# Softmax row sums taken from a 65th weight column of the value matmuls instead of from ScalarE's accumulator

## The reference, cut to what matters

```python
qkv = x @ W_qkv.T + b_qkv                       # 16 heads of 32
scores = einsum('bqhe,bkhe->bhqk', q, k) * scale
scores = where(causal, scores, -inf)
attn = softmax(scores, axis=-1)
out = einsum('bhqk,bkhe->bqhe', attn, v)
x = x + (out.reshape(b, l, d) @ W_out.T + b_out) + ffn(xn)
```

## Time and profile before

| | |
|---|---|
| median of 3 runs | 1747.48 us (1744.93 to 1747.74) |
| the profiled execution, its own time | 1748.79 us |
| its span, first to last instruction | 1747.0 us |
| busy over the span | PE 97%, weight load 78%, DVE 60%, ACT 42%, POOL 16% |
| first layer and start of the projection | 0 to about 641 us |
| projection | about 642 to 772 us |
| attention | about 772 to 1170 us |
| feed-forward net and output projection | about 1171 to 1747 us |

### The profile page before, as it was taken

How to read it: one execution, slowest core, us unless ns; L and a number is a source line. 1 busy time by engine, 2 the same in 40 slices (tenths; PEclk the granted TensorE clock), 3 DMA queues, 4 the chain that set the end, 5 groups by cost and what they waited for, 6 DMA issues and landing times. The chain is left out here.

```text
span 1747.0 us, 22877 instructions
## 1 busy us (share of the span) xinstructions
PE 1690.6 (97%) x8318; PEld 1365.9 (78%) x8318; DVE 1044.7 (60%) x1795; ACT 733.9 (42%) x1528; POOL 286.8 (16%) x280
## 2 busy tenths in 40 slices
PE   5999999999999989989999999989999999999998
PEld 3677888788788878867777777768888888888887
DVE  4321365564623454459999999964655654655776
ACT  4521322232213332249999999972222222222221
POOL 3201210310310112100000000013154031033220
PEclk9899999999999999989999999999999999999999
DMA  7200110110101038833445445514010010012243
GB/s 280 102 17 1 61 49 19 55 31 25 55 7 37 30 113 269 298 147 95 122 136 139 127 123 142 139 48 151 1 48 25 1 48 25 0 49 65 81 133 132
DMA packets 75663, 149.59 MB, mean 86 GB/s; under 512 B 9497, under 2 KB 26521, under 8 KB 74018
## 3 DMA queue, kind: packets, MB, share of 16 engines
q1 hardware_dynamic: 75554, 148.17, 27.0%
HBM read 101.87 MB, written 46.27 MB: 85 GB/s over the span
## 5 line engine op out<-in xcount | busy, mean ns | idle before, releaser
L1560 DVE TENSOR_TENSOR pt_lo<-p_turn,pt_hi 128x512 fp32r<-128x512 f32 (+3 forms) x384 | 200.8, 550 | 18.4 <-ACT pt_hi L1533 14.3
L1553 DVE TENSOR_REDUCE row_top<-p_score 128x1 f32<-128x128 f32 (+7 forms) x256 | 189.5, 750 | 15.5 <-PE p_score L1485 15.3
L1525 ACT ACTIVATE prob<-p_score,row_top 128x128 f32<-128x128 f32 (+7 forms) x256 | 190.0, 745 | 6.3 <-DVE row_top L1553 5.5
L1533 ACT ACTIVATE pt_hi<-p_turn 128x512 fp32r<-128x512 f32 (+3 forms) x384 | 182.5, 494 | 5.5 <-PE p_turn L1496 1.6
L1496 PE MATMUL p_turn<-ident,prob 128*128 128x128 f32 x1152 | 181.5, 276 | 1.3 <-DVE pt_lo L1560 1.0
L1019 DVE TENSOR_TENSOR hid<-hid,p_up 128x512 f32<-128x512 f32 x64 | 44.0, 688 | 218.7 <-PE p_up L484 203.0
L1896 DVE TENSOR_TENSOR e_hid<-e_hid,e_p_up 128x512 f32<-128x512 f32 x64 | 44.0, 687 | 196.2 <-PE e_p_up L1782 196.2
L1511 PE MATMUL p_o<-pt_hi,v 128*128 128x512 f32 (+3 forms) x384 | 148.6, 395 | 4.0 <-ACT o_both L1543 3.2
L1496 PEld LDWEIGHTS p_turn<-ident,prob 128*128 128x128 f32 x1152 | 131.8, 141 | 14.9 <-DVE pt_lo L1560 1.7
L1483 PE MATMUL p_score<-stack 128*128 128x512 f32 (+3 forms) x384 | 128.3, 389 | 7.1 <-PEq L54 3.5
L766 ACT ACTIVATE hid<-p_gate 128x512 f32<-128x512 f32 x64 | 38.3, 599 | 217.3 <-PE p_gate L484 217.2
(11 more groups left out here) (272 smaller groups left out, 4027.1 us busy)
## 6 DMA issues: line engine op xcount, KB each, us to landing
stack<-qk_parked SPq DMA_DIRECT2D x256, 128.0 KB, 3.9
raw<-in_wgu SPq DMA_DIRECT2D x64, 256.0 KB, 2.6
qk_parked<-qk SPq DMA_DIRECT2D x16, 1024.0 KB, 4.0
v_parked<-v_out SPq DMA_DIRECT2D x16, 512.0 KB, 5.6
v<-v_parked SPq DMA_DIRECT2D x8, 1024.0 KB, 9.4
o_parked<-o_both SPq DMA_DIRECT2D x64, 128.0 KB
res<-in_x SPq DMA_DIRECT2D x8, 512.0 KB
rot<-in_w2t SPq DMA_DIRECT2D x4, 1024.0 KB, 8.0
```

What stands on the lines that cost most here:

```text
L1525: act.activation(row_at(h, r, 0, width_of(r)), p_score[:, r % 2, 0:width_of(r)], ACT.Exp, bias=top[:, r:r + 1], accum_out=sums).then_inc(e ...
L1533: act.activation(pt_hi[:, (BL * h + j) % PT, c0:W], p_turn[:, (BL * h + j) % TB, c0:W], ACT.Copy).then_inc(rounded, 1)
L1553: dve.tensor_reduce(top[:, r:r + 1], p_score[:, r % 2, 0:width_of(r)], AX_X, ALU.max, negate=True).then_inc(topped, 1)
L1560: dve.tensor_tensor(pt_lo[:, slot, c0:W], p_turn[:, (BL * h + j) % TB, c0:W], pt_hi[:, slot, c0:W].bitcast(F32), ALU.subtract).then_inc(sp ...
```

## The change

The value tensors `v_out`, `v_parked` and `v` get 65 columns a head (`VC`): 32 high, 32 low, and one column of ones, which GpSimd writes once into `v_out`. `weigh` uses the 65 columns of the one head as weights, so row 64 of `p_o` holds the row sums of that head. `exp` accumulates nothing, `total` is gone, `read_o` copies 65 rows instead of 64, and SyncE stores the 65th by itself as `sum_parked`. In `layer_end` SyncE loads all sums in one load of 128 x 256 elements, VectorE inverts them after the third unit of the feed-forward net, and SyncE stores them; the transposes and the copy are gone. The pieces of a value store are 1040 bytes instead of 1024, those of a value load 8320 instead of 8192, and the spread loads of the last stage read 2048 bytes at a stretch instead of 512. Bias and scale of the projection are loaded at the end of `layer_zero` instead of at the start of the projection. `ORDER` stays as it is.

```diff
@@ -27,6 +27,7 @@
 HEADS, E = 16, 32
+VC = 2 * E + 1
@@ -306,6 +310,8 @@
                 sp.dma_start(ahead.raw[:, i], t["wqk"][0, i]).then_inc(ahead.loaded[i], 16)
+            sp.dma_start(ahead.bias[:], t["qk_bias"]).then_inc(ahead.consts, 16)
+            sp.dma_start(ahead.scale[:, 0:1], t["qk_scale"]).then_inc(ahead.consts, 16)
@@ -1205,16 +1210,16 @@
-            sp.dma_start(bias[:], qk_bias).then_inc(consts, 16)
-            sp.dma_start(scale[:], qk_scale).then_inc(consts, 16)
...
             for m in range(NT):
+                if m == 0:
+                    sp.wait_ge(one_set, 2)
...
                 b, tb = divmod(m, S // P)
-                to = v_dram.rearrange("(q b) p n -> b p q n", b=B)[b, :, :, tb * 8 * E:(tb + 1) * 8 * E]
-                sp.dma_start(to, v[:, m % BANKS].rearrange("p q h a e -> p q (h a e)").bitcast(F32))\
+                to = v_dram.rearrange("(q b) p n -> b p q n", b=B)[b, :, :, tb * 4 * VC:(tb + 1) * 4 * VC]
+                sp.dma_start(to, v[:, m % BANKS].rearrange("p q h c -> p q (h c)").bitcast(F32))\
@@ -1245,7 +1250,8 @@
             pool.memset(one[:], 1.0).then_inc(one_set, 1)
-            pool.wait_ge(one_set, 1)
+            pool.memset(v[:, :, :, :, 2 * E:].bitcast(F32), 1.0).then_inc(one_set, 1)
+            pool.wait_ge(one_set, 2)
@@ -1301,7 +1307,7 @@
                     act.wait_ge(v_stored[m % BANKS], 16 * (m // BANKS))
-                act.activation(v[:, m % BANKS, :, :, 0, :], p_v[:, m % BANKS].rearrange("p (q h e) -> p q h e", q=QUADS, h=4),
+                act.activation(v[:, m % BANKS, :, :, 0:E], p_v[:, m % BANKS].rearrange("p (q h e) -> p q h e", q=QUADS, h=4),
@@ -1332,15 +1338,15 @@
                 dve.wait_ge(v_rounded, m + 1)
-                dve.tensor_tensor(v[:, m % BANKS, :, :, 1, :], p_v[:, m % BANKS].rearrange("p (q h e) -> p q h e", q=QUADS, h=4),
-                                  v[:, m % BANKS, :, :, 0, :].bitcast(F32), ALU.subtract).then_inc(v_split, 1)
+                dve.tensor_tensor(v[:, m % BANKS, :, :, E:2 * E], p_v[:, m % BANKS].rearrange("p (q h e) -> p q h e", q=QUADS, h=4),
+                                  v[:, m % BANKS, :, :, 0:E].bitcast(F32), ALU.subtract).then_inc(v_split, 1)
...
-def attention(nc, mask, stack, v, ident, qk_dram, v_dram, o_dram, total, o_both, o_stored, qk_last, load_next):
+def attention(nc, mask, stack, v, ident, qk_dram, v_dram, o_dram, sum_dram, o_both, o_stored, qk_last, load_next):
@@ -1447,8 +1453,10 @@
                 row, t0 = E * (2 * pr + a), b * S + g * W
-                sp.dma_start(o_dram[it, :, row:row + E, t0:t0 + W], o_both[:, (G * h + g) % OS])\
-                    .then_inc(o_stored[(G * h + g) % OS], 16)
+                stored = o_stored[(G * h + g) % OS]
+                sp.dma_start(o_dram[it, :, row:row + E, t0:t0 + W], o_both[0:2 * E, (G * h + g) % OS]).then_inc(stored, 16)
+                sp.dma_start(sum_dram[TT * it + G * b + g, row // E:row // E + 1], o_both[2 * E:VC, (G * h + g) % OS])\
+                    .then_inc(stored, 16)
@@ -1506,10 +1514,10 @@
                 pe.wait_ge(split, BL * (HB * it + h) + j + 1)
-                lhs = v[:, b, kb, 2 * pr:2 * pr + 2].rearrange("p a h e -> p (a h e)")
+                lhs = v[:, b, kb, 2 * pr + a]
                 slot = (BL * h + j) % PT
-                pe.matmul(p_o[:, c0:W], lhs, pt_hi[:, slot, c0:W], start=(kb == 0), stop=False)
-                pe.matmul(p_o[:, c0:W], lhs, pt_lo[:, slot, c0:W], start=False,
+                pe.matmul(p_o[0:VC, c0:W], lhs, pt_hi[:, slot, c0:W], start=(kb == 0), stop=False)
+                pe.matmul(p_o[0:VC, c0:W], lhs, pt_lo[:, slot, c0:W], start=False,
@@ -1521,9 +1529,8 @@
                 wait(act, turned, BL * (HB * it + h - 2) + (r + 1 if r < QB else QB + r + 1))
-                sums = total[:, bass.ds(QB * G * 4 * (B * it + b) + 4 * r + 2 * pr + a, 1)]
                 act.activation(row_at(h, r, 0, width_of(r)), p_score[:, r % 2, 0:width_of(r)], ACT.Exp,
-                               bias=top[:, r:r + 1], accum_out=sums).then_inc(exped, 1)
+                               bias=top[:, r:r + 1]).then_inc(exped, 1)
@@ -1534,13 +1541,12 @@
             def read_o(it, h, g):
-                a = h % 2
...
                     act.wait_ge(*qk_last)
-                wait(act, o_stored[(G * h + g) % OS], 16 * (G * HB // OS * it + (G * h + g) // OS))
-                act.activation(o_both[:, (G * h + g) % OS], p_o[64 * a:64 * a + 64, :], ACT.Copy).then_inc(o_read, 1)
+                wait(act, o_stored[(G * h + g) % OS], 32 * (G * HB // OS * it + (G * h + g) // OS))
+                act.activation(o_both[:, (G * h + g) % OS], p_o[0:VC, :], ACT.Copy).then_inc(o_read, 1)
@@ -1680,8 +1685,8 @@
                 for h in range(4):
-                    to = raw[E * h:E * h + E, n % RING].rearrange("p (i n) -> p i n", i=J)
-                    sp.dma_start(to, spread[TT * quad + q, h:h + 1].to_broadcast([E, J, P])).then_inc(inv_in[n % RING], 16)
+                    sp.dma_start(raw[E * h:E * h + E, n % RING], inv_dram[TT * quad + q, h:h + 1].to_broadcast([E, W]))\
+                        .then_inc(inv_in[n % RING], 16)
@@ -1700,12 +1705,15 @@
                     load_res(k // 2 - 2)
-            sp.wait_ge(inv_copied, 1)
-            sp.dma_start(inv_dram.rearrange("(k p) n -> p k n", p=P), inv_t[:]).then_inc(inv_out, 16)
             for semaphore in o_stored:
-                sp.wait_ge(semaphore, 16 * (2 * HEADS * B // len(o_stored)))
+                sp.wait_ge(semaphore, 32 * (2 * HEADS * B // len(o_stored)))
+            sp.dma_start(inv_t[:], sum_dram.rearrange(flat, k=2)).then_inc(sums_in, 16)
             load_res(0)
-            for k in range(12, 12 * NG + QUADS):
+            for k in range(12, 24):
+                load_raw(k)
+            sp.wait_ge(inverted, 1)
+            sp.dma_start(inv_dram.rearrange(flat, k=2), inv_t[:]).then_inc(inv_out, 16)
+            for k in range(24, 12 * NG + QUADS):
@@ -1809,13 +1817,6 @@
                     hidden(u, c)
-                if u == 0:
-                    pe.wait_ge(inverted, 1)
-                    for i in range(2):
-                        mm = pe.transpose(p_out[:, 0, i * P:(i + 1) * P], total[:, i * P:(i + 1) * P], ident[:, :])
-                    mm.then_inc(inv_turned, 1)
-                if u == 1:
-                    pe.wait_ge(inv_copied, 1)
@@ -1850,8 +1851,6 @@
                     silu(1, 0)
-                    act.wait_ge(inv_turned, 1)
-                    act.activation(inv_t[:].rearrange("p k n -> p (k n)"), p_out[:, 0, 0:2 * P], ACT.Copy).then_inc(inv_copied, 1)
@@ -1931,7 +1930,6 @@
-            dve.reciprocal(total[:, :], total[:, :]).then_inc(inverted, 1)
@@ -1950,6 +1948,9 @@
                     add(u - 1)
+                if u == 2:
+                    dve.wait_ge(sums_in, 16)
+                    dve.reciprocal(inv_t[:], inv_t[:]).then_inc(inverted, 1)
@@ -1964,9 +1965,10 @@
     qk_dram = nc.dram_tensor("qk_parked", [HEADS // 2 * B, 2, P, S], F32, kind="Internal").ap()
-    v_dram = nc.dram_tensor("v_parked", [HEADS // 4 * B, P, 8 * S // P * E], F32, kind="Internal").ap()
+    v_dram = nc.dram_tensor("v_parked", [HEADS // 4 * B, P, 4 * S // P * VC], F32, kind="Internal").ap()
     o_dram = nc.dram_tensor("o_parked", [HEADS // 4, 2, P, T], F32, kind="Internal").ap()
-    inv_dram = nc.dram_tensor("inv_parked", [HEADS * NT, P], F32, kind="Internal").ap()
+    sum_dram = nc.dram_tensor("sum_parked", [HEADS, 4, W], F32, kind="Internal").ap()
+    inv_dram = nc.dram_tensor("inv_parked", [HEADS, 4, W], F32, kind="Internal").ap()
```

More of the change, by code:

```diff
@@ L79 @@
     done: object
+    bias: object
+    scale: object
+    consts: object
 def layer_zero(nc, t, ident, x_hi, x_lo, spare, half_turned, parked, raw_at, ahead):
@@ L1149, in load_values, with project_qkv @@
 def load_values(sp, v, v_dram, quad, b, loaded):
-    sp.dma_start(v[:, b].rearrange("p t a h e -> p (t a h e)").bitcast(F32), v_dram[B * quad + b]).then_inc(loaded, 16)
-def project_qkv(nc, wqk, wv, qk_bias, qk_scale, masks, x_hi, x_lo, qk_dram, v_dram, stack, v_first, mask, ahead, qk_parts, qk_stored):
+    sp.dma_start(v[:, b].rearrange("p t a c -> p (t a c)").bitcast(F32), v_dram[B * quad + b]).then_inc(loaded, 16)
+def project_qkv(nc, wqk, wv, masks, x_hi, x_lo, qk_dram, v_dram, stack, v_first, mask, ahead, qk_parts, qk_stored):
     QUADS = HEADS // 4
@@ L1169, in project_qkv @@
         v_lo = sb("v_lo", [P, KD, D], F32R)
-        bias = sb("bias", [P, 2 * QUADS])
+        bias, scale, consts = ahead.bias, ahead.scale, ahead.consts
         pair_bias = sb("pair_bias", [P, 2])
-        scale = sb("scale", [P, 1])
         one = sb("one", [P, 1])
@@ L1570, in gate_up_block, with layer_end @@
     return t["wgu1"][k // 8, k % 8 // 2][:, k % 2].rearrange("p k m -> p (k m)")
[L1573 removed]
+def layer_end(nc, t, x_at, x_hi, x_lo, raw, raw_in, o_stored, o_dram, sum_dram, inv_dram, parked, out):
     UNITS = TT * NG
@@ L2002, in two_layers @@
```

(10 more changed lines are left out.)

18 lines of the change are left out of this document (8 added, 10 removed).

## The result

The change makes the kernel slower by half a per cent: **1755.12 us** (median of 5 runs, 1750.98 to 1756.74) against 1746.31 us (5 runs, 1744.93 to 1747.74, two more than stood behind 1747.48), ratio 1.0048 [1.0033, 1.0063]. I had forecast 1732, and 1722 to 1744 as the range. The profiled execution took 1750.98 us, its span is 1749.1 us.

What follows compares the result with a forecast made beforehand. ScalarE was taken to set the attention's pace, TensorE the other stages'; -15.5 (attention) + 0.4 - 0.5 + 0.5 - 0.3 = -15.4 us gave a median of 1732 us, range 1722 to 1744.

Steps and rivals of the forecast that it cites:

- The step that failed: Outside the attention: TensorE never pauses and ScalarE idles, so the change counts only where TensorE waits for it.
- The accumulator's read: Attention, ScalarE: each sum's read costs 0.09 to 0.10 us; dropping them saves 0.50 us a head, -15.5 us.
- Rival D: Attention: the reads stay or cost nothing, an exponential without sum taking as long; 1747 us, chance 0.03.
- TensorE's 98.8%: Attention: TensorE's busy share, read as overlapping durations rather than a bound; its weight loads' share is 78%.
- rival A: Attention: TensorE or the fixed order is the bound after all; only -3 us, 1744 to 1747, chance 0.08.
- The 65 columns: Attention, `weigh`: narrower weights take back at most 1.1 us; counted as nothing.
- Rival C: Attention, `weigh`: 65-column weight loads aren't prefetched or packed like 128; +27 us, 1774, chance 0.06.
- more than 0.25 us apart in the middle of a pair: Attention: `weigh` matmuls spaced so would show the forecast wrong.
- Bias and scale ahead: Projection's start: earlier loads let TensorE begin sooner, limited by GpSimd's last split and the mask; -0.5 us.
- Value stores: Projection, before the mask: 1040-byte pieces carry 1.6% more bytes and delay the mask; +0.5 us.
- rival B: Projection: 1040-byte pieces need five transfers, not four, lengthening the DMA queue ahead of the mask; +7 us, 1739, chance 0.10.
- The end: Before the last phase: dropping two transposes gives -0.3 us; the last extra sum store before the barrier costs +0.4 us.

Runs made afterwards that it cites:

- e1: Changed kernel with 64 unused bytes per partition behind bias and scale, so later buffers are shifted 128 bytes: 1754.20 us, ratio 1.0044.
- e8: Changed kernel with 192 unused bytes per partition, so later buffers are shifted 256 bytes: 1735.62 us, ratio 0.9936.
- e2: Kernel before the change with only 64 unused bytes per partition ahead of the first layer's weights: 1765.00 us, ratio 1.0107.
- e4: Changed kernel with 448 unused bytes per partition, so later buffers are shifted 512 bytes: 1734.97 us, ratio 0.9932.
- e3: No model: separate streams of 96 matmuls at varied operand offsets, exponentials with and without sum, and stores of several piece lengths; matmul streams 21.77 to 22.40 us.
- e5: Kernel before the change without the exponentials' sums, the reciprocals' columns set to one: 1736.45 us.
- e11: e8 with weigh loading 128 columns of weights again instead of 65: 1737.67 us.
- e9: e8 with the mask loaded ahead of the first query weights: 1734.88 us, ratio 0.9924.
- e6: e4 with each exponential writing its sum again, into an unread scratch column: 1744.36 us.
- e12: e8 with value tiles stored two at a time, in pieces of 2080 bytes: 1737.56 us, ratio 0.9963.
- e7: No model: more matmul streams at other offsets and weight widths, and stores of 1024- and 1040-byte pieces at several pitches; store sets 24.5 to 30.3 us.

## Why the prediction was wrong

**The step that failed** is the sentence "In the other stages TensorE works without a break and ScalarE idles, so what the change does there counts only where TensorE waits for it." It puts the feed-forward nets, where TensorE never waits, at nothing, and the sum costs instructions and transfers, but no addresses. The change allocates two new tensors ahead of all later ones (the line above the gap in e1's edit), and TensorE's matmuls there start 0.233 us apart in place of 0.227, without a wait. That is +21.8 us by the count above and 19.5 by the changed kernel against e8. e1, e2, e4 and e8 settle it: the same program text at shifts of 64, 128, 256 and 512 bytes is slow, slow, fast, fast, and before at a shift of 64 is slow.

**The accumulator's read.** 0.09 to 0.10 us each on ScalarE was right: in e3, eight 512-wide exponentials with a sum start 0.66 us apart, eight without 0.57. "The head takes 11.5 to 11.7" was right as well, at 11.66, and -15.5 us measured -14.0 (400.4 to 386.4). But the cause was only two thirds right, and the number partly luck. The sum took 0.50 us a head for the reads; by themselves they bring 12.10 to 11.81, 0.29, or 9.3 us of attention (400.4 to 391.1). The rest is the low read of p_o, which I had put at "one partition more in the same instruction: nothing". It is 31 x 0.14 = 4 us. Why only 0.29 of the 0.75 us a head that ScalarE is spared gets through stays open: no run isolates the next limit. Rival D (reads that cost nothing) is out, as e5 is 10 us faster than before.

**TensorE's 98.8%** was no bound, as read from the waits: in the same 350 us it did 2383 matmuls where it had done 2316, so rival A is out. I didn't draw the second half of that warning: a busy line that hides gaps between starts doesn't show either when the starts move apart by 0.006 us.

**The 65 columns**: nothing, by e11 0.03 us a head. Rival C, the dear narrow load, is out: the load is shown as 140 ns where it was 192. (Its working takes 5 of the 24 `weigh` matmuls as uncovered already, where the part on the 65 columns has 12 such places; C's threshold doesn't hang on it.) But the forecast that TensorE's waits for exponentials shrink to a few us failed by these columns: from 785 to 1135 us its weight loads wait for them 18.7 us in e8, 0.4 in e11 with 128 columns, 3.7 in e5. With narrow loads TensorE comes to its scores earlier and waits there. The sign "more than 0.25 us apart in the middle of a pair" could tell nothing: more than half of the pairs lay further apart before the change.

**Bias and scale ahead**, -0.5: TensorE's first wait fell from 5.10 to 2.66 us and a new one of 1.65 for the last split stands at 661.85. The first matmul starts 1.41 us after GpSimd's first instruction (645.77), as forecast (643.7 - 642.23); that it reads 647.18 comes from the longer first layer. Net -0.8. But in e8 the new wait is 2.55 us, which takes back all of it: from GpSimd's first instruction to the first value matmul it is 16.70 us before, 16.08 changed, 16.70 in e8. The limit was seen rightly, GpSimd's last split; the gain is too small to be told from nothing.

**Value stores**, +0.5: from the first of them to the mask it took 47.2 us (665.69 to 712.88), now 50.8 (667.09 to 717.86), +3.6; from the first value matmul to the mask it is 53.95 and 56.01, +2.1. TensorE's wait behind it grew from 0.79 to 2.01, and is 2.37 and 2.54 in e8 and e4. So +1.2 to 1.8, above the 0.5 by bytes and far below rival B's 7. B had the direction right and, in the streams, half of the price. In e9 the wait only moved: TensorE waits for the query weights, and GpSimd, which splits them, has them only at 723.12, since their load stands behind the value stores in the same queue.

**The end**: the transposes are gone; the idle time ahead of the last phase is 4.65 against 4.40, of the forecast +0.4. Both are below what the runs can resolve.

On aligned buffers e4 and e8 take 1735.0 and 1735.6 us, against a forecast of 1732: 11 to 12 us saved, where the sum had 15.4. Part of the gap is an event of a single head: in e4 and e8 the second head takes 13.2 and 13.5 us instead of 11.66, and TensorE's granted clock stays at 1.2 GHz longer after the barrier. The windows of 14 us from the first `score` on, e8 and then the changed kernel:

```profile
771.00:785.00 14.00, 11.24 (x40) 7.85 (x41) 8.37 (x14) 8.98 (x15) 0.00 (x0) 0.50 0.16 62
```

```profile
779.00:793.00 14.00, 10.77 (x46) 7.56 (x47) 8.91 (x16) 9.62 (x16) 0.00 (x0) 0.63 0.15 59
```

PEclk is 0.50, the lower level of 1.2 GHz throughout, against 0.63. In the 4 us before either window TensorE is busy 0.5 us, since the barrier lies there. Of the profiled executions e1, e4, e6, e8 and e12 have the long second head, the others not. Why the clock comes back later in some wasn't tried, and why the start of the program gets a lower clock in some is open too.

## What to carry to other kernels

When an edit allocates, frees or resizes anything in SBUF, compare the addresses of every matmul's two operands before and after, modulo 256 bytes, for all phases behind it; 64 bytes here outweighed a whole stage's gain. A gap of unused bytes that makes them alike again is one line. If a stage that the diff doesn't touch gets longer with the same busy share and clock, count its matmuls in a window and take the distance of their starts. And when a bottleneck engine is costed, read how long after each kind of instruction the next one starts, not how long it lasts.

## What was not expected of the hardware

- float32r matmuls of 512 columns with 128 columns of weights start 0.2268 us apart when weights and moving operand are alike modulo 256 bytes, 0.2324 to 0.2343 when they are 32, 64, 96 or 128 apart, and 0.229 when the moving one is 64 ahead. Absolute places don't matter (both at 32, 64 or 256 past the grid: 0.2268).
- A ScalarE copy from PSUM partitions 64 to 127 delays the next instruction by 0.06 to 0.14 us more than one from partition 0 on: 0.13 to 0.14 us a head here, with two such copies every second head. All of them write to partitions 0 to 63.
- DMA stores in pieces of 1024 bytes at a pitch of 1040 need 24% more time than at 1024 (30.3 against 24.5 us for 8.4 MB, e7).
